# Cross attention in a decoder block: the order and size of SyncE's transfers, and preparation moved by one slot

## The chip, the cores and the metric

The kernel runs on one core of one Trainium2 chip. Times are device microseconds of one execution. Beside them one execution was taken with the hardware profiler; all rows below are of that one.

## The reference

A post-norm decoder block on x of 8 x 256 tokens x 256 features, with a context of the same shape. The part the change touches is the second of three:

```python
x = _layernorm(x + encoder(x))          # six layers of causal linear attention and an MLP
x = _layernorm(x + _L0_xattn_ref(x, ctx, ctx, ...))
x = _layernorm(x + _L0_ffn_ref(x, ...))

# _L0_xattn_ref: 16 heads of 16
q1, k1 = einsum(qh, wq1), einsum(kh, wk1); q2, k2 = einsum(qh, wq2), einsum(kh, wk2)
s1 = einsum('bshe,bthe->bhst', q1, k1) / 4;  s2 = the same of q2, k2
attn = softmax(s1) - gain * softmax(s2)
o = einsum('bhst,bthe->bshe', attn, vp)
out = normalised_per_head(o).reshape(B, S, D) @ wo.T
```

All of it is in 32-bit floats; matrix products that need it are split into a high and a low part.

## The kernel before

Encoder, cross attention and feed-forward follow each other in one program; each engine has its own instruction list, written out by hand, and they meet only in semaphores. No scheduler moves anything. In the cross attention (`cross_stage`) the work is cut into N_ALL = 64 items N: a batch b has NI = 8, for four groups of four heads and two maps (s1, s2). `slot(N)` gives b, the item's place n = 0 to 7, the next batch e = b + 1 and the previous d = b - 1. The loop body of item N, on each engine, is called slot n here.

Operands of the scores. The tile `qs` holds the queries and `ks` the keys of one batch, in two buffers, by parity of the batch. Each pair of heads takes 64 partitions, a half for each head (`a` = 0, 1), in four groups t of 16: the high, low and high parts of queries against the high, high and low parts of keys (`PARTS`: t = 0, 1, 3), and in group t = 2 a row of the negated maxima in qs against a row of ones in ks, so that the transposed scores leave PE with their maximum already subtracted. These tiles are made by way of DRAM: SP stores k_hi, k_lo to `key_rows` and q_hi, q_lo to `query_rows` (store_keys_hi, store_keys_lo, store_queries), and loads them back in the stacked layout (stack_keys, stack_queries; six loads each, of 16 partitions). stack_queries works on one half c of the heads, KC = 2 halves; stack_keys takes both halves at once. Both first write the constant rows of group 2 from the tile `unit`.

Course of an item. PE computes scores (L1272) two to three items ahead, VectorE reduces them to maxima (L1618), PE transposes these (L1279), ScalarE copies them to `mT` (L1424), and SP carries them into qs with two small DMAs (`maxima_rows`, L1146), which first wait until the item before has got its own. Then PE computes the transposed scores (L1294, two parts, pair = 0 and 1), for which it waits for those rows; ScalarE takes exp (L1447), PE multiplies by the values (L1309) and transposes every second item (L1317), VectorE normalises. scores(N + 3, 0) runs in slot N when N is odd: the first item of the next batch is met in slot 5, and it needs that batch's keys and first query half.

Preparation of batch e lies in the slots of batch b. In each slot PE does one more piece of work in the one bank `ps_j` (`side`): context transposes, x1 transposes, queries of half 0, values, queries of half 1, then the previous batch's output transposes and its two projections, in slots 0 to 7. ScalarE and VectorE empty the bank (k_hi, q_hi, values, q_lo), GpSimd normalises x1 and makes k_lo in slot 0, VectorE computes the statistics of x1 in slot 6.

SP is one in-order list: an instruction that waits holds all behind it, and its DMAs go into one queue. In slot N it does the preparation of that slot and then maxima_rows(N + 2). The preparation is: slot 1 the high keys' store; slot 2 the low ones' and the context load (256 KB each); slot 3 all of stack_keys (two constants and six loads of 128 KB) and the stores of the first query half (2 x 256 KB); slot 4 its stack (6 x 128 KB); slots 5 and 6 the same for the second half; slot 7 the input load.

## Time and profile before

| what | us |
|---|---|
| median of 3 runs | 1777.21 |
| the runs | 1775.44, 1777.21, 1781.47 |
| the profiled execution | 1771.35 |
| its span in the profile | 1769.3 |
| cross attention, first to last transposed scores | 1260.48 to 1653.20 |

The span is what the rows below are counted in; 2.05 us of the profiled execution lie outside it. The stage before (encoder) ends on PE at about 1260 us, the feed-forward follows at 1653 us. Engines are PE (matmuls), PEld (its weight loads), DVE (VectorE), ACT (ScalarE), POOL (GpSimd) and SP, whose rows, as SPq, show only the issuing of DMAs. A wait in brackets is idle time of the engine ahead of the row, with who ended it; "issue" means that the profile shows no releaser. In a view by stretch, the three last numbers are PE's granted clock as a share of full speed, the mean busy share of the 16 DMA engines, and what they moved in GB/s.

### The profile page before, as it was taken

The numbers are of one execution on the slowest core, as the hardware profiler recorded it, in microseconds if no ns is written. First come the engines' busy times: TensorE is split into PE (matmuls) and PEld (weight loads), VectorE is DVE, ScalarE is ACT, GpSimd is POOL, SyncE is SP. The second block draws the span as 40 slices with busy tenths as digits, with TensorE's granted clock in tenths as the row PEclk, the third lists the DMA queues.
The fourth block names the chain that finished last, engine by engine and source line by source line (L and its number), as shares of the span: only waits on it lengthen the run. The fifth ranks groups of instructions, "written<-read, shape, count | busy, mean of one in ns | idle before, by whom it ended". The sixth has DMA issues, their size and how long they took to land.

```text
span 1769.3 us, 38571 instructions
## 1 busy us (share of the span) xinstructions
PE 1580.0 (89%) x16078; PEld 1259.8 (71%) x16078; DVE 1254.1 (71%) x2543; ACT 957.9 (54%) x1516; POOL 784.8 (44%) x580
## 2 busy tenths in 40 slices
PE   5799999999999999999999999999856676776898
PEld 4688888888888888888888888888634444444434
DVE  4767878787877878787788778887745555654456
ACT  3455665555665655555665655554444454554445
POOL 3343555344543555344553455346323444431335
PEclk8899999999999999999999999999978888887999
DMA  6101000110010000110010000103455646444001
GB/s 117 49 1 31 7 7 23 31 31 11 25 31 27 9 8 25 31 31 11 25 31 10 22 11 25 33 2 69 91 100 96 108 86 109 86 72 68 14 1 48
DMA packets 71197, 71.55 MB, mean 40 GB/s; under 512 B 18352, under 2 KB 59248, under 8 KB 71024
## 3 DMA queue, kind: packets, MB, share of 16 engines
q1 hardware_dynamic: 71024, 69.09, 19.1%
q8 instruction: 127, 2.08, 0.5%
q14 instruction: 46, 0.38, 0.1%
HBM read 50.78 MB, written 14.68 MB: 37 GB/s over the span
## 4 chain that ended last, share of the span: by engine, by line
PE 69%; DVE 10%; SPq 6%; issue 5%; DMA 4%; ACT 4%; POOL 2%; ACTq 0%; DVEq 0%
PE e_pr L167 8%; PE e_pr L169 7%; PE e_pr L168 7%; PE e_tr L414 5%; PE e_sc L387 5%; DMA x_qs<-x_mT 3%; PE e_sc L169 3%; PE e_sc L168 3%; PE e_sc L167 3%; PE e_tr L167 3%; PE e_tr L169 3%; PE e_tr L168 3%; PE e_tr L424 2%; PE f_bank L1845 2%; PE x_psO L1309 2%
## 5 line engine op out<-in xcount | busy, mean ns | idle before, releaser
L697 POOL TENSOR_TENSOR e_h_lo<-e_h_f,e_h_hi 128x512 fp32r<-128x512 f32 x192 | 247.1, 1289 | 302.5 <-ACT e_h_hi L539 299.9
L787 DVE TENSOR_TENSOR e_am<-e_sc,c_amask 128x1024 f32<-128x1024 f32 x192 | 225.6, 1216 | 18.7 <-PE e_sc L387 18.5
L538 ACT ACTIVATE e_h_f<-e_pr,e_h_bias 128x512 f32<-128x512 f32 x192 | 132.1, 688 | 186.0 <-PE e_pr L169 182.5
L1618 DVE TENSOR_REDUCE x_mx<-x_psS 128x4 f32<-128x1024 f32 x128 | 151.5, 1219 | 112.2 <-PE x_psS L1272 112.1
L1447 ACT ACTIVATE x_ex<-x_psT 128x1024 f32<-128x1024 f32 x128 | 130.9, 1023 | 146.0 <-PE x_psT L1294 142.6
L167 PE MATMUL e_pr<-e_yT_hi,e_W_hi 128*128 128x512 f32 x384 | 168.9, 440 | 0.0
L167 PE MATMUL e_tr<-e_W_hi,e_h_hi 128*128 128x256 f32 x576 | 163.8, 284 | 0.0
L168 PE MATMUL e_tr<-e_W_lo,e_h_hi 128*128 128x256 f32 x576 | 161.6, 281 | 0.0
L169 PE MATMUL e_tr<-e_W_hi,e_h_lo 128*128 128x256 f32 x576 | 161.4, 280 | 0.0
L169 PE MATMUL e_pr<-e_yT_hi,e_W_lo 128*128 128x512 f32 x384 | 152.9, 398 | 0.0
L168 PE MATMUL e_pr<-e_yT_lo,e_W_hi 128*128 128x512 f32 x384 | 152.2, 396 | 0.0
L539 ACT ACTIVATE e_h_hi<-e_pr,e_h_bias 128x512 fp32r<-128x512 f32 x192 | 130.6, 680 | 0.0
L680 POOL TENSOR_TENSOR e_k_lo<-e_qkT,e_k_hi 128x512 fp32r<-128x512 f32 x48 | 63.7, 1348 | 143.5 <-ACT e_k_hi L548 143.5
L1294 PE MATMUL x_psT<-x_qs,x_ks 64*128 64x256 f32 x512 | 67.4, 344 | 65.2 <-DMA x_qs<-x_mT 63.1
L663 POOL TENSOR_TENSOR X<-X,e_b 128x1024 f32<-128x1024 f32 x24 | 58.1, 2421 | 134.4 <-PE e_tr L347 134.4
L167 PEld LDWEIGHTS e_tr<-e_W_hi,e_h_hi 128*128 128x128 f32 x576 | 109.2, 190 | 0.3
L169 PEld LDWEIGHTS e_tr<-e_W_hi,e_h_lo 128*128 128x128 f32 x576 | 109.1, 189 | 0.0
L168 PEld LDWEIGHTS e_tr<-e_W_lo,e_h_hi 128*128 128x128 f32 x576 | 109.0, 189 | 0.0
L414 PE MATMUL e_tr<-e_am,e_vx 128*32 128x128 f32 x3072 | 104.6, 277 | 0.0
L1272 PE MATMUL x_psS<-x_ks,x_qs 64*128 64x256 f32 x512 | 62.5, 341 | 46.2 <-issue 41.4
L1294 PEld LDWEIGHTS x_psT<-x_qs,x_ks 64*128 64x128 f32 x512 | 44.6, 213 | 82.4 <-DMA x_qs<-x_mT 67.0
L770 DVE SCALAR_TENSOR_TENSOR X<-X,e_rs,e_be 128x256 f32<-128x256 f32 x192 | 101.1, 577 | 0.0
(281 smaller groups left out, 4448.7 us busy)
## 6 DMA issues: line engine op xcount, KB each, us to landing
e_raw_m<-in_L_attn_W_dram SPq DMA_DIRECT2D x12, 1024.0 KB, 7.2
x_qs<-query_rows SPq DMA_DIRECT2D x96, 128.0 KB
x_ks<-key_rows SPq DMA_DIRECT2D x48, 128.0 KB, 5.2
query_rows<-x_q_hi SPq DMA_DIRECT2D x16, 256.0 KB, 4.9
query_rows<-x_q_lo SPq DMA_DIRECT2D x16, 256.0 KB, 5.2
x_ctok<-in_ctx_dram SPq DMA_DIRECT2D x8, 256.0 KB, 2.9
x_xo<-in_x_dram SPq DMA_DIRECT2D x8, 256.0 KB, 4.7
key_rows<-x_k_hi SPq DMA_DIRECT2D x8, 256.0 KB, 2.2
```

The costliest lines, as they stand in the source:

```text
L167: pe.matmul(out, stat[0], mov[0], start=first, stop=False)
L168: pe.matmul(out, stat[0], mov[1], start=False, stop=False)
L169: return pe.matmul(out, stat[1], mov[0], start=False, stop=last)
L414: mm = pe.matmul(out_block(s, g)[HP * a:HP * (a + 1), :], vx[:, s, h, :], am[:, s % 2, c, r, p, :], start=(s % 2 == 1 and g == 0), stop=(g ...
L538: act.activation(h_f[:, m % HR, :], ps_pr[m % 2][:, :], ACT.Gelu, bias=h_bias[:, m:m + 1])
L539: act.activation(h_hi[:, m, :], ps_pr[m % 2][:, :], ACT.Gelu, bias=h_bias[:, m:m + 1]).then_inc(gelu_done, 1)
L697: pool.tensor_tensor(h_lo[:, m, :], h_f[:, m % HR, :], h_hi[:, m, :].bitcast(F32), ALU.subtract).then_inc(h_lo_done, 1)
L770: dve.scalar_tensor_tensor(x, x, rs[i][:, s:s + 1], bias[:, :], ALU.mult, ALU.add).then_inc(ln_done[i], 1)
L787: dve.tensor_tensor(am[:, s % 2, c, :, :, :], ps_sc[:, :, c * 2 * P:(c + 1) * 2 * P].rearrange("p r (h n) -> p r h n", n=P), amask[:, :].u ...
L1294: mm = pe.matmul(ps_t[:, a, c * S:(c + 1) * S], ks[j][rows, 2 * g + pair, blk(c)], qs[j][rows, 2 * g + pair, k, :], start=True, stop=True, ...
L1447: act.activation(ex[:, N % 2, pair].rearrange("p a c n -> p (a c n)"), ps_t[:, :, :].rearrange("p a n -> p (a n)"), ACT.Exp).then_inc(ex_d ...
L1618: dve.tensor_reduce(mx[:, N % 2, :, 0:HG].rearrange("p i (a h) -> p h a i", a=2)[:, pair], ps_s[pair][:, :, :].rearrange("p a (i j) -> p a ...
```

## The change

SP now sends the rows of the maxima ahead of each slot's preparation (maxima_rows(N + 1) at the head of slot N), and the preparation is divided differently among the slots. stack_keys takes one half c of the heads (64 KB loads), and both stack functions can issue a part of their six loads (`steps`), in an order (`STACK`) that alternates the two partition halves. The constant rows are written once for each buffer, before the loop (`fixed_rows`); of the queries' only the maxima's row itself is reset from batch 2 on, as before. PE waits for the keys of a half with the queries of that half. All preparation from the context transposes on comes one slot earlier: the context of batch b + 2 is transposed in slot 7 of batch b (batch 1's before the loop), x1 in slot 0, and so on, and the output transposes always in slot 4, projections in 5 and 6. GpSimd's x1 and k_lo move to slot 7, VectorE's q_lo to slots 1 and 3, its statistics of x1 behind the maxima in slot 6.

```diff
             cross.scores(1, 1)
             cross.maxima(1)
             cross.scores(2, 0)
+            pe.wait_ge(z_done[2], SB * NT * L)
             cross.items()
...
-    LOADS = 2 * len(PARTS) + 2
+    STACK = [(a, part) for part in PARTS for a in range(2)]
...
+    def keys_arrived(n):
+        return 16 * (len(STACK) * n + 4 * min((n + 1) // 2, 2))
+
+    def queries_arrived(n):
+        return 16 * (len(STACK) * n + 2 * max(n - 2 * KC, 0))
...
-        def stack_keys(e):
-            wait(sp, t_full, 2 * NI * (e - 1))
+        def fixed_rows(e):
             sp.wait_ge(sets_done, 3)
-            wait(sp, ks_loaded, 16 * LOADS * e)
+            if e > 0:
+                sp.wait_ge(ks_loaded, keys_arrived(KC * e))
             for a in range(2):
-                sp.dma_start(ks[e % 2][half_rows(a, 2), :, :].bitcast(F32),
+                sp.dma_start(ks[e][half_rows(a, 2), :, :].bitcast(F32),
                              unit[0:DH, :].unsqueeze(1).broadcast_to([DH, PAIRS, S])).then_inc(ks_loaded, 16)
-            sp.wait_ge(k_stored, 32 * e + 32)
-            for a in range(2):
-                for t, _, low in PARTS:
-                    part = key_rows[e, low].rearrange("c (r a d) n -> a d (c r) n", a=2, d=DH)[a]
-                    sp.dma_start(ks[e % 2][half_rows(a, t), :, :].bitcast(F32), part).then_inc(ks_loaded, 16)
+                sp.dma_start(qs[e][half_rows(a, 2), :, :, :].rearrange("p r k n -> p (r k) n").bitcast(F32),
+                             unit[DH:2 * DH, :].unsqueeze(1).broadcast_to([DH, PAIRS * MAPS, S])).then_inc(ks_loaded, 16)
+
+        def stack_keys(e, c, steps=STACK):
+            n = KC * e + c
+            pairs = slice(PC * c, PC * (c + 1))
+            if steps[0] == STACK[0]:
+                wait(sp, t_full, 2 * NI * (e - 1))
+                if n > 0 and n != KC:
+                    sp.wait_ge(ks_loaded, keys_arrived(n))
+                sp.wait_ge(k_stored, 32 * e + 32)
+            for a, (t, _, low) in steps:
+                part = key_rows[e, low, c].rearrange("(r a d) n -> a d r n", a=2, d=DH)[a]
+                sp.dma_start(ks[e % 2][half_rows(a, t), pairs, :].bitcast(F32), part).then_inc(ks_loaded, 16)
...
-        def stack_queries(e, c):
+        def stack_queries(e, c, steps=STACK):
             n = KC * e + c
             pairs = slice(PC * c, PC * (c + 1))
-            wait(sp, t_full, 2 * NI * (e - 1))
-            wait(sp, qs_loaded, 16 * LOADS * n)
-            lanes = DH if e < 2 else 1
-            for a in range(2):
-                sp.dma_start(qs[e % 2][half_rows(a, 2, lanes), pairs, :, :].rearrange("p r k n -> p (r k) n").bitcast(F32),
-                             unit[DH:DH + lanes, :].unsqueeze(1).broadcast_to([lanes, PC * MAPS, S])).then_inc(qs_loaded, 16)
-            sp.wait_ge(q_stored, 32 * n + 32)
-            for a in range(2):
-                for t, low, _ in PARTS:
-                    part = query_rows[e, low, c].rearrange("(r a d) m -> a d r m", a=2, d=DH)[a]
-                    sp.dma_start(qs[e % 2][half_rows(a, t), pairs, :, :].rearrange("p r k n -> p r (k n)").bitcast(F32), part).then_inc(qs_loaded, 16)
+            if steps[0] == STACK[0]:
+                wait(sp, t_full, 2 * NI * (e - 1))
+                wait(sp, qs_loaded, queries_arrived(n))
+                for a in range(2 if e >= 2 else 0):
+                    sp.dma_start(qs[e % 2][half_rows(a, 2, 1), pairs, :, :].rearrange("p r k n -> p (r k) n").bitcast(F32),
+                                 unit[DH:DH + 1, :].unsqueeze(1).broadcast_to([1, PC * MAPS, S])).then_inc(qs_loaded, 16)
+                sp.wait_ge(q_stored, 32 * n + 32)
+            for a, (t, low, _) in steps:
+                part = query_rows[e, low, c].rearrange("(r a d) m -> a d r m", a=2, d=DH)[a]
+                sp.dma_start(qs[e % 2][half_rows(a, t), pairs, :, :].rearrange("p r k n -> p r (k n)").bitcast(F32), part).then_inc(qs_loaded, 16)
...
         load_input(0)
         load_context(1)
         store_keys_hi(0)
+        fixed_rows(0)
         store_keys_lo(0)
-        stack_keys(0)
+        for c in range(KC):
+            stack_keys(0, c)
         load_input(1)
         for c in range(KC):
             store_queries(0, c)
             stack_queries(0, c)
         maxima_rows(0)
-        maxima_rows(1)
-        load_input(2)
+        fixed_rows(1)
         for N in range(N_ALL):
             b, n, e, d, after, before = slot(N)
+            if N + 1 < N_ALL:
+                maxima_rows(N + 1)
+            if after and n == 0:
+                store_keys_hi(e)
+                store_keys_lo(e)
             if after and n == 1:
-                store_keys_hi(e)
+                stack_keys(e, 0)
+                if e + 1 < B:
+                    load_input(e + 1)
             if after and n == 2:
-                store_keys_lo(e)
+                store_queries(e, 0)
+            if after and n == 3:
+                stack_queries(e, 0, STACK[:4])
+            if after and n == 4:
+                stack_queries(e, 0, STACK[4:])
+                stack_keys(e, 1, STACK[:3])
                 if e + 1 < B:
                     load_context(e + 1)
-            if after and n == 3:
-                stack_keys(e)
-                store_queries(e, 0)
-            if after and n == 4:
-                stack_queries(e, 0)
             if after and n == 5:
                 store_queries(e, 1)
             if after and n == 6:
-                stack_queries(e, 1)
-            if n == 7 and e + 2 < B:
-                load_input(e + 2)
-            if N + 2 < N_ALL:
-                maxima_rows(N + 2)
+                stack_queries(e, 1, STACK[:4])
+            if after and n == 7:
+                stack_queries(e, 1, STACK[4:])
+                stack_keys(e, 1, STACK[3:])
...
-            if n == 0 and pair == 0:
-                pe.wait_ge(ks_loaded, 16 * LOADS * (b + 1))
             if k == 0 and pair == 0 and g % 2 == 0:
-                pe.wait_ge(qs_loaded, 16 * LOADS * (KC * b + g // 2 + 1))
+                pe.wait_ge(ks_loaded, keys_arrived(KC * b + g // 2 + 1))
+                pe.wait_ge(qs_loaded, queries_arrived(KC * b + g // 2 + 1))
...
         def side(N):
 
             b, n, e, d, after, before = slot(N)
             if after and n == 0:
-                pe.wait_ge(q_lo_done, KC * e)
-                wait(pe, z_done, QB * (b - 1))
-                context(e, ps_j)
+                x1_transpose(e, ps_j)
             if after and n == 1:
-                x1_transpose(e, ps_j)
+                queries(e, 0, ps_j)
             if after and n == 2:
-                queries(e, 0, ps_j)
-            if after and n == 3:
                 pe.wait_ge(q_lo_done, KC * e + 1)
                 values(e, ps_j)
-            if after and n == 4:
+            if after and n == 3:
                 pe.wait_ge(v_done, e + 1)
                 queries(e, 1, ps_j)
             if not after and n < 2 * KC:
@@ -1342,16 +1356,21 @@
                     pe.wait_ge(q_lo_done, KC * B)
                     pe.wait_ge(z_done, QB * (B - 2))
                 ffn.rows_in(n // KC, n % KC, ps_j)
-            if before and project_slot(n, after) == -1:
+            if before and n == 4:
                 if after:
                     pe.wait_ge(q_lo_done, KC * e + 2)
                 else:
                     ffn.rows_taken()
                 out_transpose(d)
-            if before and 0 <= project_slot(n, after) < QB:
-                out_project(d, (project_slot(n, after),))
+            if before and n in (5, 6):
+                out_project(d, (n - 5,))
+            if n == 7 and b + 2 < B:
+                pe.wait_ge(q_lo_done, KC * e + 2)
+                wait(pe, z_done, QB * b)
+                context(b + 2, ps_j)
 
         def items():
+            context(1, ps_j)
             for N in range(N_ALL):
...
             maxima(0)
             maxima(1)
+            context(1, ps_j[:, :])
...
@@ -1465,19 +1485,19 @@
                     out_copy((N - 2) // 2)
                 exps(N, 1)
                 if after and n == 0:
-                    context(e, ps_j[:, :])
+                    x1_transposed(e)
                 if after and n == 1:
-                    x1_transposed(e)
+                    queries_hi(e, 0)
                 if after and n == 2:
-                    queries_hi(e, 0)
+                    values(e, ps_j[:, :])
                 if after and n == 3:
-                    values(e, ps_j[:, :])
-                if after and n == 4:
                     queries_hi(e, 1)
                 if not after and n in (0, KC):
                     ffn.rows_in(n // KC, ps_j[:, :])
-                if before and n == (5 if after else 4):
+                if before and n == 4:
                     out_transposed(d)
+                if n == 7 and b + 2 < B:
+                    context(b + 2, ps_j[:, :])
...
         def items():
+            x1_norm(1)
+            keys_lo(1)
             for N in range(N_ALL):
                 b, n, e, d, after, before = slot(N)
-                if after and n == 0:
-                    x1_norm(e)
-                    keys_lo(e)
...
                 if n == 4 and b + 2 < B:
                     encoder_scale(b + 2)
                     encoder_add(b + 2)
+                if n == 7 and b + 2 < B:
+                    x1_norm(b + 2)
+                    keys_lo(b + 2)
...
         def items(also):
+            x1_stats(1)
             for N in range(N_ALL):
                 b, n, e, d, after, before = slot(N)
                 if N % 2 and N >= 3:
                     normalise((N - 3) // 2)
-                if N == 0:
-                    x1_stats(1)
...
                     encoder_stats(b + 2)
-                if n == 6 and b + 2 < B:
-                    x1_stats(b + 2)
                 if N in also:
                     also[N]()
                 if N + 2 < N_ALL:
                     maxima(N + 2, 1)
                 if N + 3 < N_ALL:
                     maxima(N + 3, 0)
-                if after and n == 2:
+                if after and n == 1:
                     queries_lo(e, 0, ps_j[:, :])
-                if after and n == 4:
+                if after and n == 3:
                     queries_lo(e, 1, ps_j[:, :])
                 if not after and n in (1, KC + 1):
                     ffn.rows_in(n // KC, ps_j[:, :])
-                if before and (5 if not after else 6) <= n < (7 if not after else 8):
-                    residual(d, (n - (6 if after else 5),))
+                if n == 6 and b + 2 < B:
+                    x1_stats(b + 2)
+                if before and n in (5, 6):
+                    residual(d, (n - 5,))
```

SP's list, before, in batch 1, which prepares batch 2: from the low keys' store in slot 2 to the maxima rows behind slot 4 (x_mT is the tile of the maxima, x_unit the constants; two DMAs of x_mT belong to one item):

```order
L1103 DMA key_rows<-x_k_lo 128x2x256
L1088 DMA x_ctok<-in_ctx_dram 128x2x256
L1146 DMA x_qs<-x_mT 1x2x256 x2
L1110 DMA x_ks<-x_unit 16x8x256 x2
L1116 DMA x_ks<-key_rows 16x8x256 x6
L1121 DMA query_rows<-x_q_hi 128x512
L1123 DMA query_rows<-x_q_lo 128x512
L1146 DMA x_qs<-x_mT 1x2x256 x2
L1132 DMA x_qs<-x_unit 1x8x256 x2
L1138 DMA x_qs<-query_rows 16x4x512 x6
L1146 DMA x_qs<-x_mT 1x2x256 x2
```

and after, in the same batch, from slot 1 to slot 4:

```order
L1132 DMA x_ks<-key_rows 16x4x256 x6
L1099 DMA x_xo<-in_x_dram 128x2x256
L1161 DMA x_qs<-x_mT 1x2x256 x2
L1137 DMA query_rows<-x_q_hi 128x512
L1139 DMA query_rows<-x_q_lo 128x512
L1161 DMA x_qs<-x_mT 1x2x256 x2
L1148 DMA x_qs<-x_unit 1x8x256 x2
L1153 DMA x_qs<-query_rows 16x4x512 x4
L1161 DMA x_qs<-x_mT 1x2x256 x2
L1153 DMA x_qs<-query_rows 16x4x512 x2
L1132 DMA x_ks<-key_rows 16x4x256 x3
L1095 DMA x_ctok<-in_ctx_dram 128x2x256
```

Before, ten large DMAs stand between two pairs of x_mT in slot 3 and six in slot 4; after, seven at most, with six of these (the keys of one half, in slot 1) half as large.

PE's list, before, slot 0 of batch 1 and the start of slot 1 (x_psT the transposed scores, x_psJ the bank of the side work, x_ctok the context):

```order
L1294 MATMUL x_psT<-x_qs,x_ks 128x256 x4
L1309 MATMUL x_psO<-x_ex,x_vx 32x256 x8
L1272 MATMUL x_psS<-x_ks,x_qs 128x256 x4
L1294 MATMUL x_psT<-x_qs,x_ks 128x256 x4
L1272 MATMUL x_psS<-x_ks,x_qs 128x256 x4
L1209 MATMUL x_psJ<-c_ident,x_ctok 128x128 x4
L1279 MATMUL x_psS<-c_ident,x_mx 128x128 x2
L1294 MATMUL x_psT<-x_qs,x_ks 128x256 x4
L1317 MATMUL x_psO<-c_ident,x_oS 128x128 x4
L1272 MATMUL x_psS<-x_ks,x_qs 128x256 x8
L1294 MATMUL x_psT<-x_qs,x_ks 128x256 x4
L1209 MATMUL x_psJ<-c_ident,x_x 128x128 x4
```

and after, slot 7 of batch 0 and the following slot 0:

```order
L1338 MATMUL x_psO<-c_ident,x_oS 128x128 x4
L1293 MATMUL x_psS<-x_ks,x_qs 128x256 x8
L1315 MATMUL x_psT<-x_qs,x_ks 128x256 x4
L1231 MATMUL x_psJ<-c_ident,x_ctok 128x128 x4
L1330 MATMUL x_psO<-x_ex,x_vx 32x256 x8
L1300 MATMUL x_psS<-c_ident,x_mx 128x128 x2
L1315 MATMUL x_psT<-x_qs,x_ks 128x256 x4
L1330 MATMUL x_psO<-x_ex,x_vx 32x256 x8
L1293 MATMUL x_psS<-x_ks,x_qs 128x256 x4
L1315 MATMUL x_psT<-x_qs,x_ks 128x256 x4
L1293 MATMUL x_psS<-x_ks,x_qs 128x256 x4
L1231 MATMUL x_psJ<-c_ident,x_x 128x128 x4
```

The context transposes stand one slot earlier, and the x1 transposes take their place in slot 0; around them nothing else moves.

## Rows read from the trace of the kernel before

**Rows 1.** The page, busy time of each engine and its share.
```profile
PE 1580.0 (89%) x16078; PEld 1259.8 (71%) x16078; DVE 1254.1 (71%) x2543; ACT 957.9 (54%) x1516; POOL 784.8 (44%) x580
```

**Rows 2.** PE's waits, 1260 to 1655 us: in total, times, longest.
```profile
PE x_psT L1294 <- DMA x_qs<-x_mT: 63.1, 14, 6.5
PE x_psS L1272 <- issue: 41.4, 7, 6.5
```

**Rows 3.** Busy time by stretch: batch 2 and batch 7; columns in the first line.
```profile
core 0: us, PE busy (x) PEld busy (x) DVE busy (x) ACT busy (x) POOL busy (x), PEclk, DMA share, GB/s
...
1364.48:1415.78 51.30, 35.68 (x324) 23.18 (x325) 28.52 (x52) 25.37 (x35) 21.92 (x16) 0.83 0.55 94
1621.69:1653.20 31.51, 29.66 (x279) 17.95 (x279) 20.73 (x37) 21.34 (x28) 9.88 (x6) 0.95 0.07 16
```

**Rows 4.** The same view: stores, key loads, query loads of batch 2.
```profile
1376.00:1378.00 2.00, 1.35 (x10) 0.75 (x8) 2.00 (x3) 1.24 (x3) 1.74 (x1) 1.00 0.85 252
1381.00:1387.00 6.00, 4.94 (x56) 2.85 (x52) 5.15 (x11) 4.45 (x7) 5.05 (x6) 1.00 1.01 136
1394.00:1398.00 4.00, 0.00 (x0) 0.00 (x0) 1.25 (x2) 0.00 (x0) 0.00 (x0) 0.50 1.08 127
```

**Rows 5.** Timeline, slots 2 and 3 of batch 2: start, duration, engine, line.
```profile
1373.24 0.50 PE L1294 MATMUL x_psT<-x_qs,x_ks 64*128 64x256 f32 x4
...
1373.80 1.16 SPq L1146 DMA_DIRECT2D x_qs<-x_mT  x2
...
1377.73 0.50 PE L1294 MATMUL x_psT<-x_qs,x_ks 64*128 64x256 f32 x4
...
1378.75 0.74 PE L1272 MATMUL x_psS<-x_ks,x_qs 64*128 64x256 f32 x8
```

**Rows 6.** Timeline, slots 4 and 5 of batch 2; waits in brackets.
```profile
1380.95 4.85 SPq L1116 DMA_DIRECT2D x_ks<-key_rows  x6
...
1382.24 0.50 PE L1294 MATMUL x_psT<-x_qs,x_ks 64*128 64x256 f32 x4
...
1386.84 1.31 SPq L1146 DMA_DIRECT2D x_qs<-x_mT  x2
...
1391.13 0.80 PE L1294 MATMUL x_psT<-x_qs,x_ks 64*128 64x256 f32 x4 [5.19 <-DMA x_qs<-x_mT]
```

**Rows 7.** Timeline, slots 5, 6 and 7 of batch 2.
```profile
1391.94 2.67 SPq L1138 DMA_DIRECT2D x_qs<-query_rows  x6
...
1400.18 0.80 PE L1272 MATMUL x_psS<-x_ks,x_qs 64*128 64x256 f32 x4 [6.48 <-issue]
...
1404.31 0.50 PE L1294 MATMUL x_psT<-x_qs,x_ks 64*128 64x256 f32 x4
...
1407.94 0.50 PE L1294 MATMUL x_psT<-x_qs,x_ks 64*128 64x256 f32 x4
```

**Rows 8.** Timeline, from slot 7 of batch 1 into batch 2.
```profile
1357.27 0.41 DVE L1648 TENSOR_TENSOR x_z<-x_psJ,x_x 128x256 f32<-128x256 f32 x1
...
1359.10 1.25 SPq L1146 DMA_DIRECT2D x_qs<-x_mT  x2
...
1364.48 0.50 PE L1294 MATMUL x_psT<-x_qs,x_ks 64*128 64x256 f32 x4 [3.28 <-DMA x_qs<-x_mT]
```

**Rows 9.** The page, DMA issues: KB each, us from issue to landing.
```profile
key_rows<-x_k_hi SPq DMA_DIRECT2D x8, 256.0 KB, 2.2
```

**Rows 10.** Timeline of SP's queue before batch 0.
```profile
1216.24 0.37 SPq L1099 DMA_DIRECT2D key_rows<-x_k_hi  x1
...
1223.67 1.42 SPq L1110 DMA_DIRECT2D x_ks<-x_unit  x2
```

**Rows 11.** PE's waits, 1236 to 1256 us.
```profile
PE x_psS L1272 <- DMA x_qs<-query_rows: 4.5, 1, 4.5
```

**Rows 12.** Timeline, slots 0 and 2 of batch 2.
```profile
1367.42 1.11 PE L1209 MATMUL x_psJ<-c_ident,x_ctok 128*128 128x128 f32 x4
...
1375.28 0.69 DVE L1641 TENSOR_REDUCE x_om<-x_sq 128x32 f32<-128x512 f32 x1 [1.65 <-POOL x_sq L1534]
```

2 lines of the change are left out of this document (removed).

## Prediction

> **What bounds the kernel now.** I read the page first: PE is busy 89% of the span [rows 1], so the question is where the remaining time is lost. The list of PE's waits in the cross attention (1260 to 1655 us) names two kinds of long wait and hardly anything else: 63.1 us in 14 waits of the transposed scores for the rows of the maxima, and 41.4 us in 7 waits of at most 6.5 us in front of the scores, labelled "issue" [rows 2]. Two and one, so three to a batch, for seven batch boundaries (0/1 to 6/7). The third reading is by batch: batch 2 goes from 1364.48 to 1415.78 us, 51.3 us, with PE busy 35.7 us at a granted clock of 0.83; the last batch, for which nothing is prepared, takes 31.5 us for the same eight slots, at 0.95 [rows 3]. The fourth is the DMA rate: loads that stack rows into qs or ks run at 127 to 136 GB/s with the DMA engines' share at 1.0, while a store with the context load reaches 252 GB/s [rows 4]. So a 128 KB stacking load takes 1.0 us, however deep the queue, and a 256 KB store or context 1.04 us.
>
> An undisturbed slot is the measure for everything below [rows 5]. Slot 2 starts at 1373.24, SP issues the rows of the maxima 0.56 us later in two DMAs (1.16 us), slot 3 starts at 1377.73: 4.49 us, no DMA wait. I take 4.4 us as a slot, a tenth less because VectorE waits in slot 2 for something that moves (below). The rows issued early in slot N are needed at the start of slot N+1, so they have 8.8 us counted from the start of slot N-1, whose preparation is what lies ahead of them in the queue.
>
> The three stalls, seen in one batch: **Into slot 5.** Slot 3 queues 1 MB of key loads and constants and then 0.5 MB of query stores. The key loads alone keep SP until 1385.80; with slot 4 begun at 1382.24 it could have sent the rows at 1382.8, sends them at 1386.84, and they land behind the backlog: slot 5 starts at 1391.13, PE idle 5.19 us [rows 6]. **Within slot 5.** PE's scores of the next batch's first item need that batch's first query stack; its six loads are only issued from 1391.94, and PE stands 6.48 us until 1400.18 [rows 7]. **Into the next batch.** The rows wait behind 0.75 MB of the second query stack: sent at 1359.10, slot 0 starts at 1364.48, PE idle 3.28 us [rows 8]. That is 14.95 us of 51.3.
>
> **The change part by part.**
>
> *The order "maxima first" alone: nothing.* maxima_rows(N+1) ahead of slot N's preparation is the same cyclic order as maxima_rows(N+2) behind it. What differs is what lies between two pairs of rows.
>
> *The packets.* Per batch SP now puts in: slot 0, both key stores (2.1 us of queue time); slot 1, six 64 KB key loads and the input (3 + 1 = 4); slot 2, two stores (2.1); slot 3, four query loads (4); slot 4, two query loads, three 64 KB key loads and the context (2 + 1.5 + 1 = 4.5); slot 5, two stores (2.1); slot 6, four loads (4); slot 7, two and three (3.5). Sum 26.3 us, in eight slots of 4.4 = 35.2. A key store takes 2.2 us from issue to landing [rows 9], 1.04 of it data, so data begins 1.2 us after issue. In slot 3: rows sent at 0.56, done at 1.72, two small constant DMAs (1.4 us of issue, as the pair in [rows 10]), data from 4.3 to 8.3; the next rows land at about 8.4, needed at 8.8. Slot 4's queue starts at 8.4 - 4.4 = 4.0: its two query loads end at 6.0, that is 1.6 us into slot 5, and the scores of the next batch want them at about 1.4 (in slot 3 the eight scores matmuls begin at 1378.75, 1.0 after its start, and the second four are meant) [rows 5]. Then keys and context to 8.5, rows at 8.6, needed at 8.8. Slot 6 is slot 3 again, with 0.4 us to spare, and less if slot 6 itself is short (3.63 us in the trace, 1404.31 to 1407.94 [rows 7]). Slot 1 ends at 2.9 + 4 = 6.9. So the three stalls go, but with 0.2 to 0.4 us of margin in three places and some 0.2 missing in one. I leave a rest of 1.0 us a batch; its bounds are 0 and, if every one of the four loaded slots is late by 1 us, 4 us.
>
> *Constants written once.* The 16 unit rows of ks (two loads of 128 KB) vanish from each batch: 2 us less of the queue, in slot 3, where it counts; contained in the sum above. For both buffers they are now sent before the loop, 768 KB each. The first set fills a gap: after the store of the high keys at 1216.24 SP has nothing to issue until the low ones are there, and starts the constants at 1223.67 [rows 10]. The first query stack had four constants of 128 KB ahead of it in the queue, so it arrives some 4 us earlier, and PE's wait of 4.5 us for it [rows 11] all but goes. The second set goes out behind the first maxima rows, 6 us of queue; the second rows, needed one slot (4.6 us) after slot 0 begins, just clear it. I count 3.5 us of gain, between 0 and 4.5, with the next edit taken off.
>
> *Preparation one slot earlier.* The PE items keep their number, eight a batch, one in each slot; each is preceded by the one it was preceded by before, so no new neighbour in bank psJ. The context transposes of batch 1 (1.11 us, [rows 12]) move in front of slot 0 and are paid openly, 1 us once, since slot 0 has one item again (x1). New waits: PE's context in slot 7 waits for the residual of slot 6; queued behind it are attend and the transposed maxima. In the trace VectorE ran the residual of slot 6 at 1357.27 (0.41 us), at the very start of slot 7 [rows 8]; the x1 statistics now stand in front of it, so it ends about 1.9 us into slot 7, and PE comes to its context at 2.0 to 2.2: nothing, at worst 0.3 us a batch. GpSimd normalises x1 behind it, until about the slot's end, before PE's x1 transposes 2 us into slot 0. VectorE's q_lo moves from slots 2 and 4 to 1 and 3, which also hold the normalisation; it sits in a gap before the next maxima, so nothing. In slot 2 VectorE stood 1.65 us, until 1375.28, for GpSimd's squares [rows 12], which run behind x1 and the low keys that now lie in slot 7: 0.5 us a batch of that I take as gain (0 to 0.9).
>
> *What stalls leave behind.* Without its wait slot 5 lasted 13.18 - 6.48 = 6.7 us, at half clock and with every engine starting cold; slots 4 and 6 were short in exchange (3.70 and 3.63). Against 4.4 each that nets 2.3 - 0.7 - 0.8 = 0.8 us a batch.
>
> **The sum.** A batch: 51.3 - 14.95 - 0.8 - 0.5 + 1.0 = 36.1 us, 15.2 less. Seven of them 106.4, and 3.5 at the start: 110 us. The profiled execution took 1771.35 us (span 1769.3), so 1661; it was 5.9 us under the median of the runs, 1777.21, so the median should come to 1667 us.
>
> A rule against the interleaving of halves, and a row: one key stack of six loads ran at 136 GB/s although consecutive loads in it go to different groups of 16 partitions [rows 4]; so alternating halves won't be faster than that and I give it nothing. The Trainium skill, "DMA: Bandwidth & Descriptors", Rules for kernel authors, says the same of two transfers to disjoint halves: they serialize. Its page "SBUF — State Buffer", on the port swizzle, gives bandwidth by how many of 16 ports the partitions reach; 16 partitions reach four, an estimate of 109 GB/s (the rows show somewhat more), and two halves eight. By that rule loads in flight together could go twice as fast, the rest of 1.0 us a batch would be gone, and the sum would give 1660; the trace speaks for the first.
>
> **The rivals.**
> 1. *The rows stay late in loaded slots.* For it: the margins above are a few tenths, and SP's issues sometimes take longer with a deep queue. Against: 26 us of 35 are used. 4 to 8 us a batch, 28 to 56 in all, less the 7 counted: 1688 to 1716, say 1700.
> 2. *The slots themselves become shorter.* Slots of the last batch took 31.5/8 = 3.94 us at a clock of 0.95 [rows 3]; half way to it (4.17, no rest) is 33.4 a batch, 19 us more gained: 1648.
> 3. *Each added DMA costs its start.* Twelve key loads instead of six; if the 1.2 us before data [rows 9] did not overlap, 7.2 us a batch, 50 us: 1717. Against: in rows 4 six loads follow each other at a share of 1.01. The skill's page on DMA (Anatomy of one DMA) puts about 2.0 us fixed on each; paid in line that would be 84 us and 1751; no row shows it paid in line.
> 4. *No gain.* The waits reappear in other slots, as many in sum, since PE then waits for each pair of rows: 8 x 1.9 us. That needs a queue that is never empty; 9 us a batch are free. 1775.
> 5. *Slower.* The smaller, alternating loads run much slower than 1.0 us per 128 KB. The queue decides from the point where a batch's DMA time passes 51.3 us: 8.3 us of other work and 18 units of load at 2.4 us. At 2.9 us it is 60.5 us, 9.2 more, seven times: 1842. Against: 1 KB rows of keys and 2 KB rows of queries ran alike [rows 4].
>
> **How the numbers follow.** Forecast 0.60 (1655 to 1688), rival 1 0.20, rival 2 0.12, rival 3 0.03, rival 4 0.02, rival 5 0.03. The range that holds 8 in 10 takes the forecast's, most of rival 2 and half of rival 1: 1645 to 1702. A measurement of this kernel tells 0.3%, 5 us, from no change. Faster by more: 0.60 + 0.20 + 0.12 + 0.03 = 0.95; same 0.02; slower 0.03.
>
> **What would show it.** Right: PE's waits for the maxima rows under 10 us in all (63.1 now), its "issue" waits in front of the scores under 7 us (41.4), batches 35 to 37 us apart, clock above 0.93 over the stage, no PE wait for the first query stack. Rival 1: many waits of 1 to 2 us for the maxima rows, slots 3, 4 and 6. Rival 2: batches near 33 us. Rivals 3 and 5: gaps in the DMA share, or a rate under 100 GB/s, within a stack. Wrong altogether: a new line high in PE's waits, such as the context behind x_z.

## The result, and the profile after

| kernel | median, us | runs | against before | 95% interval |
|---|---|---|---|---|
| before | 1777.35 | 1775.44 to 1781.47 | | |
| after | 1679.96 | 1677.79 to 1681.22 | 0.9448 | 0.9428 to 0.9468 |

The change saves 97 us, 5.5%. The profiled execution after took 1678.82 us, its span is 1677.1; the span before was 1769.3, so 92.2 us of span are to be found. The forecast was 1667 (1661 for the profiled execution, 110 us less); the time lies within 1645 to 1702, 13 us above the forecast.

The page first. Same work, as many instructions on each engine, but less busy time on PE than in [rows 1]:

```profile
PE 1566.9 (93%) x16078; PEld 1251.7 (75%) x16078; DVE 1259.3 (75%) x2543; ACT 957.5 (57%) x1516; POOL 784.8 (47%) x580
```

PE's waits in the cross attention (1255 to 1600 us; total, times, longest), to be laid beside [rows 2]:

```profile
PE x_psT L1315 <- DMA x_qs<-x_mT: 18.3, 14, 2.6
...
PE x_psS L1300 <- DVE x_mx L1640: 6.7, 17, 1.3
PE x_psO L1330 <- DVE x_o L1655: 3.9, 7, 0.7
PE x_psJ L1231 <- POOL x_x L1540: 2.9, 1, 2.9
PE x_psS L1293 <- DMA x_ks<-key_rows: 1.7, 2, 1.1
```

The 63.1 us for the rows of the maxima are 18.3, in as many places (14) but none over 2.6 us. The 41.4 us of "issue" in front of the scores are gone without a trace. New, and small, are a wait for x_o in each slot 7 and one for x_x in the first slot.

By stretch (us, busy time and count of PE, PEld, DVE, ACT, POOL, then clock, DMA share, GB/s): batches 2 and 7 after, as [rows 3], then batches 1 to 6 together, after and, in the second fence, before.

```profile
1339.70:1377.64 37.94, 33.37 (x324) 21.32 (x324) 29.50 (x54) 25.26 (x35) 22.00 (x17) 0.96 0.60 121
1529.10:1560.10 31.00, 29.48 (x279) 18.39 (x279) 20.56 (x35) 21.43 (x28) 9.98 (x5) 0.94 0.12 21
1303.83:1529.10 225.27, 199.08 (x1940) 127.59 (x1940) 173.44 (x301) 150.91 (x209) 119.68 (x86) 0.95 0.55 120
```

```profile
1313.16:1621.69 308.53, 216.50 (x1944) 139.41 (x1944) 169.48 (x300) 151.97 (x210) 119.45 (x86) 0.83 0.53 92
```

Six batches take 83.3 us less, 13.9 each. Of these, 17.4 us are PE's own busy time (216.5 to 199.1 for the same matmuls), since the granted clock rose from 0.83 to 0.95 when the long waits went; the other 65.8 are idle time. The rest of the 92.2: batch 0 is 11.4 shorter (52.7 to 41.3 us), the last batch 0.5, but the first transposed scores come 2.0 us later (1262.52 for 1260.48), and what follows the last transposed scores takes 0.9 more (117.0 for 116.1). 83.3 + 11.4 + 0.5 - 2.0 - 0.9 = 92.3.

All of this is one execution of each kernel. A second profiled execution of the same kernel (after_again, below) has 38.5 us for batch 0 in place of 41.3 and 38.1 in place of 37.5 for each of the next six, so the mean of the six is known to some 0.6 us, and batch 0 only to 3 us.

Where the remaining waits stand: timeline of slots 3 to 5 of batch 2 (slot 3 begins at 1351.46).

```profile
1352.27 1.18 SPq L1161 DMA_DIRECT2D x_qs<-x_mT  x2
...
1353.54 1.36 SPq L1148 DMA_DIRECT2D x_qs<-x_unit  x2
...
1354.94 1.84 SPq L1153 DMA_DIRECT2D x_qs<-query_rows  x4
1356.01 0.51 PE L1315 MATMUL x_psT<-x_qs,x_ks 64*128 64x256 f32 x4
...
1356.89 1.22 SPq L1161 DMA_DIRECT2D x_qs<-x_mT  x2
...
1361.96 1.18 SPq L1161 DMA_DIRECT2D x_qs<-x_mT  x2
1361.99 0.50 PE L1315 MATMUL x_psT<-x_qs,x_ks 64*128 64x256 f32 x4 [2.27 <-DMA x_qs<-x_mT]
```

The rows issued at 1356.89 stand behind four query loads. My working gave the loads' data until 8.3 us after the slot's start, 1359.8, and the rows right behind. The four 1 KB packets of these rows were in fact moved from 1359.34 to 1359.60, a little earlier than that. But PE saw them at 1361.96, 2.3 us later: their last completion is recorded at 1361.94. In a slot without loads ahead it is complete 0.3 us after its packets (rows issued at 1352.27, packets 1353.47 to 1354.17, last completion 1354.46). The loads themselves are as late: the fourth one's last packet ended at 1359.55, its last completion came at 1361.27, 1.7 us later, and the rows' came next. This is no single case. There are fourteen places in this trace where rows stand behind four loads; in twelve of them the completion came 1.7 to 2.3 us after the rows' packets, in the other two 0.5 and 1.0. So a small transfer behind such loads into 16 partitions pays not only for their data but, in most places, also for a landing of some 2 us after its own packets. I had put 0.1 us there.

The wait costs a second time, in slot 5. That slot lasts 6.0 us (1361.99 to 1368.00), where the last batch has 4.5 for it, and there is no long wait inside it. PE works in it at half clock for a part of the time:

```profile
1364.50:1366.60 2.10, 2.10 (x9) 1.27 (x12) 2.10 (x3) 1.02 (x1) 0.43 (x1) 0.50 0.72 265
```

The start: SP's queue after, to be laid beside [rows 10], and PE's wait of [rows 11] as it is now.

```profile
1217.89 0.37 SPq L1106 DMA_DIRECT2D key_rows<-x_k_hi  x1
1218.62 0.78 SPq L1117 DMA_DIRECT2D x_ks<-x_unit  x1
...
1220.82 2.12 SPq L1119 DMA_DIRECT2D x_qs<-x_unit  x1
1224.89 0.36 SPq L1110 DMA_DIRECT2D key_rows<-x_k_lo  x1
1228.42 7.04 SPq L1132 DMA_DIRECT2D x_ks<-key_rows  x12
...
1239.55 3.13 SPq L1153 DMA_DIRECT2D x_qs<-query_rows  x6
```

```profile
PE x_psS L1293 <- DMA x_qs<-query_rows: 4.3, 1, 4.3
```

The constants filled the gap and ran over it: 768 KB from 1218.62 on, the last landed at 1228.17. The low keys' store, issued behind them, landed at 1228.41, and everything after it (twelve key loads, 7 us of issue, with a wait between the halves; query stores; query loads) is late by as much as the constants were to save. The wait is 4.3 us where it was 4.5. Of the 2.0 us by which the stage begins later, 1.65 are there before any of this: the high keys' store went out at 1217.89, at 1216.24 before [rows 10], behind an encoder that the change doesn't touch. Counted from that store the first transposed scores come after 44.6 us, 44.2 before: no gain, and the loss is 0.4.

### The profile page after: what moved, and what is told of

Read it like the earlier page. It is cut to its first block, busy times and chain, and to the rows that moved or that the text cites. A ratio compares the mean times of both kernels' runs of the same rounds, so it can differ in the third digit from the quotient of the medians.

```text
span 1677.1 us, 38614 instructions
## 1 busy us (share of the span) xinstructions
PE 1566.9 (93%) x16078; PEld 1251.7 (75%) x16078; DVE 1259.3 (75%) x2543; ACT 957.5 (57%) x1516; POOL 784.8 (47%) x580
## 4 chain that ended last, share of the span: by engine, by line
PE 73%; DVE 10%; SPq 5%; DMA 4%; ACT 4%; issue 3%; POOL 1%; ACTq 0%; DVEq 0%; POOLq 0%
PE e_pr L167 8%; PE e_pr L169 7%; PE e_pr L168 7%; PE e_tr L414 6%; PE e_sc L387 5%; PE e_sc L167 3%; PE e_sc L168 3%; PE e_sc L169 3%; PE e_tr L167 3%; PE e_tr L169 3%; PE e_tr L168 3%; DMA x_qs<-x_mT 3%; PE e_tr L424 3%; PE x_psO L1330 2%; PE f_bank L1866 2%
## 5 line engine op out<-in xcount | busy, mean ns | idle before, releaser
L167 PEld LDWEIGHTS e_pr<-e_yT_hi,e_W_hi 128*128 128x128 f32 x384 | 72.5, 189 | 32.4 <-issue 13.9
L764 DVE SCALAR_TENSOR_TENSOR X<-X,e_mv,e_g 128x256 f32<-128x256 f32 x192 | 93.1, 544 | 0.0
L414 PEld LDWEIGHTS e_tr<-e_am,e_vx 128*32 128x32 f32 x3072 | 78.6, 110 | 15.6 <-issue 12.3
```

What stands on the lines that cost most here:

```text
L167: pe.matmul(out, stat[0], mov[0], start=first, stop=False)
L414: mm = pe.matmul(out_block(s, g)[HP * a:HP * (a + 1), :], vx[:, s, h, :], am[:, s % 2, c, r, p, :], start=(s % 2 == 1 and g == 0), stop=(g ...
L764: dve.scalar_tensor_tensor(x, x, mv[i][:, s, 0:1], gain[:, :], ALU.subtract, ALU.mult).then_inc(xc_done[i], 1)
```

## The experiments

Twelve kernels. Times are medians; the ratio is to the kernel before on the same chip (1773 to 1777 us). "Rows wait" is PE's wait for the maxima's rows in the cross attention (total / places); "batches" is the mean of batches 1 to 6.

| run | us | ratio, interval | rows wait | batches |
|---|---|---|---|---|
| after | 1679.96 | 0.9448, 0.9428 to 0.9468 | 18.3 / 14 | 37.5 |
| after_again | 1678.25 | 0.9469, 0.9450 to 0.9487 | 18.9 / 13 | 38.1 |
| q_half | 1646.09 | 0.9277, 0.9248 to 0.9306 | 3.3 / 6 | 33.1 |
| tail_quarter | 1669.07 | 0.9405, 0.9373 to 0.9436 | 14.4 / 15 | 36.1 |
| split33 | 1669.09 | 0.9404, 0.9381 to 0.9428 | 7.4 / 13 | 36.6 |
| stats_first | 1676.89 | 0.9445, 0.9417 to 0.9472 | 23.6 / 15 | 37.8 |
| unsplit | 1713.31 | 0.9673, 0.9656 to 0.9689 | 45.6 / 16 | 43.0 |
| half_major | 1685.99 | 0.9515, 0.9498 to 0.9531 | 24.1 / 16 | 39.0 |
| act_queue | 1710.89 | 0.9654, 0.9639 to 0.9670 | 9.8 / 11 | 42.5 |
| const_spread | 1671.68 | 0.9407, 0.9393 to 0.9422 | 19.8 / 17 | 37.8 |
| reset_early | 1654.34 | 0.9308, 0.9294 to 0.9323 | 4.7 / 7 | 34.5 |
| before_const | 1764.43 | 0.9927, 0.9909 to 0.9945 | 47.6 / 14 | 49.9 |
| combined | 1643.64 | 0.9268, 0.9246 to 0.9290 | 3.8 / 7 | 33.6 |

### Less data in the queue: q_half and tail_quarter

```diff
+                some = slice(PC * c, PC * c + (2 if e > 1 else PC))
-                sp.dma_start(qs[...][half_rows(a, t), pairs, :, :]..., part)
+                sp.dma_start(qs[...][half_rows(a, t), some, :, :]..., part[:, 0:some.stop - some.start, :])
```

What isn't loaded stays stale, so q_half leaves out half of the queries' data. In tail_quarter the 2 is a 1, and the condition holds only for the last two loads of a stack.

> The changed kernel, but from batch 2 on each of the six query loads brings two of its four pairs of heads, 64 KB in place of 128 KB (the rest of the queries is stale). The queue's time in slots 3 and 6 falls from 4 to 2 us. Theory A, that the maxima rows wait for the loads ahead of them in the queue (drained) plus some 2 us until those writes are acknowledged: PE's waits for the maxima rows (18.3 us in all in the changed kernel) fall under 4 us for batches 2 to 7, a batch takes 34 to 35 us in place of 37.7, the kernel 1660 to 1664. Theory B, that something else than the queue makes slots 4, 5 and 7 long (VectorE's order, half clock): batches stay above 36.5 us, 1675 or more.

> The changed kernel, but from batch 2 on the last two query loads of each half, issued in slots 4 and 7 behind the maxima rows, bring one pair of heads in four, 32 KB in place of 128 KB (the rest is stale). What lies ahead of the maxima rows is untouched. Theory A (rows held by what is ahead of them, and 2 us of late acknowledgement): PE's wait at the start of slot 5 stays at 1.5 to 2.5 us a batch and the one at the next batch's start near 1 us; only slot 5 itself gets shorter (6.0 to 5.0), 1672 to 1677. Theory C (rows held by the loads sent behind them, which fill the same ports until they have landed): both waits go, 1664 to 1669.

With half the bytes of the query loads of batches 2 to 7 (0.75 MB less for each) 15 of the 18.3 us of waiting go and a batch takes 33.1 us: 34 us less in all, 27 of them in batches 1 to 6, more than expected. With only the last two loads cut, slots 4 and 7 are relieved by 1.5 us each, but 14.4 us of waits stay in 15 places, as Theory A has it. The time, 1669, does not fit A (1672 to 1677); it lies at the end of what C gave (1664 to 1669), though C's sign, that both waits go, failed. So the loads in slots 3 and 6, ahead of the rows, seem to count for most, and those behind them for a part. Neither run says whether data or landing is the larger part.

### Other cuts of the same data: split33 and unsplit

```diff
             if after and n == 3:
-                stack_queries(e, 0, STACK[:4])
+                stack_queries(e, 0, STACK[:3])
             if after and n == 4:
-                stack_queries(e, 0, STACK[4:])
-                stack_keys(e, 1, STACK[:3])
+                stack_queries(e, 0, STACK[3:])
...
             if after and n == 5:
                 store_queries(e, 1)
+                stack_keys(e, 1, STACK[:3])
             if after and n == 6:
-                stack_queries(e, 1, STACK[:4])
+                stack_queries(e, 1, STACK[:3])
             if after and n == 7:
-                stack_queries(e, 1, STACK[4:])
+                stack_queries(e, 1, STACK[3:])
```

> The changed kernel with the six query loads of a half divided 3 and 3 instead of 4 and 2 over slots 3/4 and 6/7, and the first three key loads of the second half moved from slot 4 to slot 5. Theory A: one load less ahead of the rows, so the waits at slot 5 and at the next batch lose 1 us each, slot 5's wait for the stack stays; 1.5 to 2 us a batch, 1668 to 1671. Theory C: one load more behind the rows, so these waits grow by up to 1 us: 1680 to 1690.

At 3 us of loads in each slot in place of 4 the rows' waits fall from 18.3 to 7.4 us, none over 1.5. But the third load of the second part now arrives after the scores that need it: PE's waits list has a line that after does not have.

```profile
PE x_psS L1293 <- issue: 9.3, 7, 2.1
```

These waits (9.3 us) are nearly what the rows' have lost (10.9), and still the kernel is 10.9 us faster; a part of that is PE's own time, 197.0 us at a clock of 0.97 in batches 1 to 6, where it was 199.1 at 0.95. The opposite, in unsplit: `stack_keys(e, 0)` and `stack_keys(e, 1)` whole in slot 1, `stack_queries` whole in slots 3 and 6.

> The changed kernel with its preparation one slot earlier, its constants written once and its rows first, but the loads undivided: both halves' key loads (twelve of 64 KB) together in slot 1, the six query loads of a half whole in slots 3 and 6. Only the division of the loads is undone. My theory (a slot's queue must leave some 2 us beside its data, since the rows land 2 us after their packets): slots 1, 3 and 6 each queue 6 us of loads (slot 1 with the input 7) in a slot of 4.4, so each makes the rows late by 2 to 4 us; waits for the rows of the maxima 7 x 7 us, about 50 in all against 18.3 now, batches 41 to 43 us, 1705 to 1720. Rival (the order of the rows and the constants are what pays, a division within the load phase is worth little because the queue drains in the light slots): batches 38 to 39 us, 1680 to 1690.

```profile
PE x_psT L1311 <- DMA x_qs<-x_mT: 45.6, 16, 5.1
```

1713 us and 45.6 us of waits, as the late landing said (1705 to 1720, about 50). So dividing the loads is worth 2.0 to 2.3 of the 5.5%; the other 3.3% come from rows first, preparation one slot earlier and constants once, together. In this run too there is no wait of the scores for queries, and in before_const (next) they all stay, so it was neither the division nor the keys' constants that removed those 41.4 us.

### One cost by itself: before_const

```diff
-            wait(sp, ks_loaded, 16 * LOADS * e)
-            for a in range(2):
+            wait(sp, ks_loaded, keys_arrived(e))
+            for a in range(2 if e < 2 else 0):
                 sp.dma_start(ks[e % 2][half_rows(a, 2), :, :]..., unit[0:DH, :]...)
```

> The kernel before with one part of the change alone: the unit rows of ks (two loads of 128 KB) go out only with the first key stack of each buffer, not in slot 3 of every batch. My sum had counted them at 2 us of queue in slot 3. Theory: slot 3's backlog is 2 us shorter from batch 1 on, and the two waits in slot 5 both stand at its end, so six batches get 2 us shorter: 12 us, a ratio of 0.993. Rival (the query stack of slot 4 takes over: its start is set by the stores, not by the keys): no change, 0.998 to 1.002.

0.9927: 13 us by the ratio, 12.2 by the two medians (1776.61 and 1764.43), where 12 were expected. By the spans it is 6.4 us, but the profiled execution of before was a fast one, 6.0 under its median, so the medians are the better measure. The scores' "issue" waits stay, and the rows' shrink from 63.1 by 15.5, not all of which reaches the time, since PE is busy 222.1 us in batches 1 to 6 at a clock of 0.81, where it was 216.5 at 0.83. PE's waits from 1260 to 1655 us:

```profile
PE x_psT L1297 <- DMA x_qs<-x_mT: 47.6, 14, 5.8
PE x_psS L1275 <- issue: 41.8, 7, 6.5
```

### Who is late in slot 7: stats_first

```diff
                     encoder_stats(b + 2)
+                if n == 6 and b + 2 < B:
+                    x1_stats(b + 2)
                 if N in also:
...
-                if n == 6 and b + 2 < B:
-                    x1_stats(b + 2)
                 if before and n in (5, 6):
```

> The changed kernel with VectorE's statistics of x1 put back ahead of the maxima of slot 6, as they stood before the change. If the new place costs (PE waits 3.9 us in 7 waits for VectorE's x_o in slot 7, 0.2 us in 1 wait before): those waits go and slot 7 gets 0.5 us shorter, 1675 to 1678. Rival: the maxima of slot 6 come 1.3 us later and slot 6 pays what slot 7 gets: 1679 to 1682.

In after VectorE runs the x1 statistics and then the residual at the start of slot 7, ahead of the normalisation that PE waits for:

```profile
1372.26 0.74 DVE L1606 BATCH_NORM_STATS2 x_st<-x_xw 128x6 f32<-128x256 f32 x2
...
1373.40 0.42 DVE L1670 TENSOR_TENSOR x_z<-x_psJ,x_x 128x256 f32<-128x256 f32 x1
...
1374.47 0.60 DVE L1655 SCALAR_TENSOR_TENSOR x_o<-x_tmp,x_neg_gain 128x128 f32<-128x128 f32 x1
...
1375.22 1.07 PE L1330 MATMUL x_psO<-x_ex,x_vx 128*32 128x256 f32 x16 [0.68 <-DVE x_o L1655]
```

With the statistics ahead of the maxima the wait for x_o falls from 3.9 us to 0.5, and the one for the rows rises from 18.3 to 23.6. The median of 1676.9 lies where the theory had it, but it can't be told from that of after (0.9445 against 0.9448 and 0.9469), and the waits side with the rival. The wait had cover: whoever passes PE's x_o earlier stands for the rows longer.

### The order within a stack: half_major

```diff
-    STACK = [(a, part) for part in PARTS for a in range(2)]
+    STACK = [(a, part) for a in range(2) for part in PARTS]
```

> The changed kernel with one edit: the six loads of a stack go first to the three groups of one half, then to those of the other, in place of alternating (the cuts after four, two and three loads stay where they are). My theory (loads in one queue run one after the other at 127 to 136 GB/s whichever partitions they go to): same time within 0.3%, 1680. Rival (two loads to different halves of the partitions overlap and share more of the write side, so alternating them is what makes them fast): each stack loses a tenth to a half of its rate, 0.4 to 2 us in each of four loaded slots, 11 to 50 us in all, and the DMA share and GB/s in the stretches of the loads fall.

> The changed kernel itself once more, so that the other kernels have it beside them on the same chip: 0.945 of the kernel before, within 0.3%; waits for the rows of the maxima about 18 us in some 14 places.

1686 us, ratio 0.9515 against 0.9469 on the same chip: 0.5% slower, with intervals that just do not touch, and 24.1 us of waits for 18.9. My theory (no difference) is wrong by a little. In the load phase of slot 3, batch 2, the same 3.5 us (from 4.0 to 7.5 after the slot's start), first after, then half_major:

```profile
1355.46:1358.96 3.50, 3.50 (x46) 2.10 (x38) 3.12 (x9) 2.72 (x4) 1.52 (x3) 1.00 0.87 141
```

```profile
1351.07:1354.57 3.50, 3.50 (x46) 2.10 (x38) 3.12 (x9) 2.72 (x4) 1.52 (x3) 1.00 0.92 135
```

Over these windows of batches 1 to 6 the mean is 147 and 141 GB/s, single ones lie between 134 and 159 and between 118 and 155. So two loads to different halves in flight together gain some 4% at most by this measure, which is less than the spread of the windows, and not the double that the prediction works out from ports. The Trainium skill, "DMA: Bandwidth & Descriptors", Rules for kernel authors, has them serialize, and the trace agrees up to these 4%.

### Another queue for the rows: act_queue

```diff
             copy(mT[0:HG, N % 2, :], ps_s[1][0:HG, 0, 0:S], mT_tr, N + 1, mT_done)
...
+            if n == 0:
+                act.wait_ge(ks_loaded, keys_arrived(KC * b + 1))
+            if k == 0 and g % 2 == 0:
+                act.wait_ge(qs_loaded, queries_arrived(KC * b + g // 2 + 1))
+            wait(act, rows_set, 32 * N)
+            act.wait_ge(mT_done, N + 1)
+            for a in range(2):
+                act.dma_start(qs[b % 2][HALF * a + DH * 2:HALF * a + DH * 2 + 1, 2 * g:2 * g + 2, k, :].bitcast(F32),
+                              mT[2 * a:2 * a + 2, N % 2, :].bitcast(F32)).then_inc(rows_set, 16)
...
-        maxima_rows(0)
...
-            if N + 1 < N_ALL:
-                maxima_rows(N + 1)
```

> The changed kernel with the rows of the maxima issued by ScalarE into its own DMA queue, right behind its copy of the transposed maxima, instead of by SyncE; all loads and stores stay in SyncE's queue. Theory A1 (rows land late because they stand in one queue behind loads, each waiting for the completion of the one before): in a queue of their own they land within 2 us of issue whatever SyncE has queued; waits for the rows fall from 18 us to under 5, batches 35 to 36 us, though ScalarE pays about 0.9 us of issue in each slot, which it has (it is busy half the time); about 1665. Rival A2 (the lateness sits in the DMA engines, which serve all queues: the rows' packets and write receipts share them with the loads): waits stay at 10 to 18 us, time 1675 to 1685. Rival A3 (ScalarE's issue time, and its wait for earlier rows, hold up the exps): waits of PE for x_ex or for maxima appear, 1685 or more.

1711 us. The third case decides the time: ScalarE's issue stands between the copy and the exp, and PE pays for it in every slot. With slots that much longer, the 9.8 us of waits for the rows can't decide between the first two (under 5, or 10 to 18).

```profile
PE x_psT L1303 <- ACT x_ex L1465: 66.6, 80, 2.5
PE x_psT L1303 <- DMA x_qs<-x_mT: 9.8, 11, 1.6
```

What the run was for can be read all the same, in slots 3 to 5 of batch 2, ScalarE's issues and PE's wait:

```profile
1375.24 1.16 ACTq L1460 DMA_DIRECT2D x_qs<-x_mT  x2
...
1381.82 0.50 PE L1303 MATMUL x_psT<-x_qs,x_ks 64*128 64x256 f32 x4 [1.36 <-DMA x_qs<-x_mT]
```

In a queue of their own, with nothing ahead of them in it, the rows take 6.5 us, since SyncE's six query loads had been issued just before. Their four packets (1 KB, in the second queue) moved from 1378.91 to 1379.84, from 3.7 us after the issue on, and their last completion came at 1381.78, 1.9 us after the packets. So the lateness doesn't come from the order within one queue; it lies in what both queues share, and its second part is the completion. The Trainium skill, "DMA: Bandwidth & Descriptors", Queues, rings and completion order, states that the increment of a semaphore is a strongly ordered write, which lands only after every earlier write of that DMA engine, across its queues. That fits both this run and after: the last of SyncE's query loads was complete at 1380.96 here and at 1361.27 there, and the rows' completions came next, up to 1381.78 and 1361.94. The rule itself no run here shows apart from other causes.

### The constants: const_spread

```diff
-        fixed_rows(0)
+        fixed_keys(0)
+        fixed_queries(0, 0)
         store_keys_lo(0)
-        for c in range(KC):
-            stack_keys(0, c)
+        stack_keys(0, 0)
+        store_queries(0, 0)
+        fixed_queries(0, 1)
+        stack_queries(0, 0)
+        stack_keys(0, 1)
         load_input(1)
-        for c in range(KC):
-            store_queries(0, c)
-            stack_queries(0, c)
+        store_queries(0, 1)
+        fixed_keys(1)
+        stack_queries(0, 1)
         maxima_rows(0)
-        fixed_rows(1)
+        fixed_queries(1, 0)
```

`fixed_rows` is cut into its keys' part and one part for each half of the queries; fixed_queries(1, 1) goes out in slot 2 of batch 0.

> The changed kernel with the constant rows sent in pieces: of buffer 0 only 512 KB (keys both halves, queries one half) in the gap ahead of the low keys' store, the last 256 KB behind the first query stores; the second key stack of batch 0 behind the first query stack; buffer 1's in three pieces (256 KB each) behind the second query stores, behind the first maxima rows, and in slot 2. Theory (the early wait of 4.3 us for the first query stack stayed because 768 KB of constants overran a gap of 4.7 us, and batch 0's slots 0 and 1 are 7.2 us each because the second 768 KB stand in front of the rows and the key stores): the wait falls to under 1.5 us, slots 0 and 1 of batch 0 to 4 to 5.5 us; 3 for the wait and 4 for the slots, 7 us in all, 1671. Rival (the wait is set by the chain query stores, landing, loads, whose start the low keys and PE's own work set, not by the constants): the wait stays over 3 us and slot 0 over 6; 1676 to 1680.

Half right. PE's wait for the first query stack is gone (a wait of 1.7 us for keys stands in its place), the first transposed scores come at 1256.79 instead of 1262.52 (40.6 us behind the high keys' store instead of 44.6, so 4.1 of the 5.7 us belong to the edit), and the time is 1672 us, 0.9407 against 0.9448 and 0.9469. But slots 0 and 1 of batch 0 are as long as before this edit, 7.21 and 6.83 us, although no constants stand in front of the rows. In slot 0 it is another wait:

```profile
1260.04 2.43 POOL L1548 TENSOR_SCALAR x_x<-x_xw,x_mv,x_rs 128x256 f32<-128x256 f32 x2
...
1262.52 1.11 PE L1239 MATMUL x_psJ<-c_ident,x_x 128*128 128x128 f32 x4 [2.36 <-POOL x_x L1548]
```

Batch 1's x1 is now transposed in slot 0, and GpSimd normalises it only after VectorE's last statistics of the encoder. Slot 1 is long for another reason. It holds no long wait, but PE does its work in it at half clock:

```profile
1269.74:1276.87 7.13, 7.02 (x40) 3.99 (x39) 4.44 (x7) 3.17 (x5) 0.00 (x0) 0.50 0.41 129
```

This is slot 1 in after. In q_half, whose instructions are the same up to here, the clock was 0.82 in it and it took 4.78 us. So the wait in slot 0 costs up to 2.4 us more behind it, in some executions. The late x1 is a cost of the shift which I had not seen: I had costed it for the batches in the middle, where GpSimd has slot 7 for it, and batch 1 has no slot 7 ahead of it. The edit also puts the keys' second stack behind the first query stack, so how much of the earlier start is due to the constants isn't separated here.

### Two tiny DMAs: reset_early

```diff
             if after and n == 2:
                 store_queries(e, 0)
+                reset_maxima(e, 0)
...
             if after and n == 5:
                 store_queries(e, 1)
+                reset_maxima(e, 1)
```

`reset_maxima` is what stood at the head of stack_queries: two waits and the two DMAs from `unit`.

> The changed kernel with one step moved: the two small DMAs that reset the maxima's row in qs (8 KB each, 1.4 us of issue) go out behind the query stores of slots 2 and 5 instead of ahead of the query loads in slots 3 and 6. Same bytes, same packets. Theory (what makes the rows late in slots 4 and 7 is where the load phase ends, plus 2 us of landing): the loads' data start and end 1.4 us earlier, slots 4 and 7 shorten by 1.0 to 1.4 us in the six batches that have resets; 12 to 15 us less, 1663 to 1666, waits for the rows from 18 to about 7. Rival (SyncE's issue isn't what sets the start of the loads; the stores' landing does, or the slot in which the time is saved passes it to slot 5): under 5 us, 1675 to 1680.

The clearest run. The same packets but for the place of four 8 KB transfers a batch, and the time falls from 1679 to 1654 us (0.9308), more than the 12 to 15 expected. Slots 3 and 4 of batch 2 (slot 3 begins at 1346.21):

```profile
1347.02 1.22 SPq L1165 DMA_DIRECT2D x_qs<-x_mT  x2
...
1348.28 1.81 SPq L1157 DMA_DIRECT2D x_qs<-query_rows  x4
...
1351.32 1.17 SPq L1165 DMA_DIRECT2D x_qs<-x_mT  x2
...
1354.40 0.50 PE L1322 MATMUL x_psT<-x_qs,x_ks 64*128 64x256 f32 x4
```

The loads are issued 2.07 us after the slot's start, 3.48 in after, and the wait of 2.27 us is none. Over the stage, and over batches 1 to 6:

```profile
PE x_psT L1322 <- DMA x_qs<-x_mT: 4.7, 7, 1.0
```

```profile
1299.69:1506.51 206.82, 192.24 (x1942) 122.94 (x1942) 171.37 (x296) 151.47 (x209) 120.03 (x85) 0.99 0.59 130
```

Waits for the rows of 14.2 us are gone (18.9 in after_again, 4.7 here), somewhat more than the 11 expected. The rest of the excess is PE's own time: for batches 1 to 6 it is busy 192.2 us at a clock of 0.99, against 201.9 at 0.94 in after_again, 9.7 us less. These batches are 21.8 us shorter (228.7 and 206.8), so 12.1 of that are idle time; the spans differ by 25.4 (1677.7 and 1652.3). For each us of waiting that went, PE's busy time fell by some 0.8 us with it.

### What the runs point to: combined

The edits of const_spread, reset_early and stats_first, the context load from slot 4 to slot 5, and for batch 1:

```diff
             for s in range(SB):
                 cross.maxima(s // 2, s % 2)
+                if s == SB - 1:
+                    cross.x1_stats(1)
...
             cross.encoder_add(1)
+            cross.x1_norm(1)
             rsqrt(2, ve_done[2], NT * L)
```

Both had been the first line of their engine's `items`.

> The changed kernel with what the runs so far point to, all of it complete: the constant rows in pieces; the resets of the maxima's row behind the query stores of slots 2 and 5; the context load from slot 4 to slot 5; VectorE's statistics of batch 1's x1 ahead of the last residual of the encoder and GpSimd's normalisation of it ahead of the encoder's last power, in place of the head of the item loops; VectorE's later x1 statistics ahead of slot 6's maxima. If landing time behind full load phases was the limit, each part adds up, since the queue now has slack: resets alone gave 1652 in span; constants 5; x1 of batch 1 without PE's wait of 2.9 and slots 0 and 1 near 5 in place of 7.2, 4; slot 5 without the context 0.8 in six batches, 5; waits for x_o 3: 1635 in span, about 1637, a ratio of 0.922. Rival (as with the statistics alone, a wait taken away in one place comes back as a wait for the rows): 1648 to 1655.

1643.64 us, 0.9268: the fastest of all, 2% under after, 130 us under before, with nothing left out. It lies between the two expectations. What was said of batch 1 holds: slots 0 and 1 take 4.79 and 4.78 us, the wait for x_x is gone. What wasn't foreseen is that the keys come late in place of the rows:

```profile
PE x_psS L1311 <- DMA x_ks<-key_rows: 5.2, 7, 1.2
PE x_psT L1333 <- DMA x_qs<-x_mT: 3.8, 7, 0.9
```

```profile
1291.12:1492.92 201.80, 190.02 (x1941) 121.70 (x1940) 170.94 (x296) 150.91 (x210) 119.18 (x84) 1.00 0.56 134
```

PE is busy 190.0 of 201.8 us, 94%, at the full clock; the queue holds it up for only some 9 us in the whole stage. The five edits were taken together, so what each is worth beside the others isn't known.

## Why the prediction was nearly right

*What bounds the kernel, and that it goes.* Right. The three stalls of a batch (14.95 us) were the cost, and the two kinds of wait fell from 104.5 us to 18.3. The clock over batches 1 to 6 is 0.95, the batches 35.9 to 39.0 us; "35 to 37" was too narrow. Of the five signs that were to show it right, two held (no "issue" waits in front of the scores, clock above 0.93) and three failed: waits for the rows under 10 us (18.3), batches of 35 to 37, no wait for the first query stack (4.3). That the time came within 13 us is in part luck: errors below pull both ways.

*The order alone, nothing; the constants, 2 us of queue a batch.* The second is shown by before_const (13 us for 12; the interval is 0.55% to 0.91% of the time). The first was not tried alone.

*A rest of 1.0 us a batch.* This is the step that was mis-sized. It had the data of each slot's queue right (8.3 us, and the packets moved 8.1 after the slot's start), but took "the next rows land at about 8.4" from it. They land some 2 us after their packets when loads into 16 partitions are in front, at 10.5 in the slot shown. The waits measured 18.3 us, 2.6 a batch instead of 1.0; the margins of 0.2 to 0.4 us were no margins. The rows that I had taken the landing from could not show it: a key store's 2.2 us [rows 9] are 1.2 of start and 1.04 of data, but nothing stands ahead of it. The trace of before has it in another place, which I had quoted for its length alone: in [rows 8] the rows stand behind six query loads; 369 of the loads' 384 packets had ended by 1362.62 (the last at 1363.84), and the rows were complete at 1364.44. Rival 1 (rows late in the loaded slots, waits of 1 to 2 us in slots 3, 4 and 6) was true in kind, at a third of its price. What the rest of 1.0 us left out besides is the clock: a wait of 2.3 us is followed by a slot 5 partly at half clock, and reset_early shows some 0.8 us of PE's time for each us of waiting.

*Preparation one slot earlier: nothing, at worst 0.3 a batch.* Waits for x_o of 3.9 us in seven slots 7, which stats_first shows to be covered by those for the rows; and for batch 1's x1, once, slots 0 and 1 of 7.2 and 7.1 us where they had been 4.6 and 5.5, which nothing in the prediction held. const_spread took away the cause that I had suspected, and it stayed; combined took away this one as well, and it went. So batch 0 gained 11.4 instead of 15.2 (14.2 by the second execution).

*Slots of 4.4 us.* Slots 0 and 2 of most batches are now 3.63 us, where I kept 4.4 in slot 0 and took 0.5 off in slot 2. Rival 2 was true for these two slots, and they made up for part of the rest. In all a batch in the middle gained 13.9 us, not 15.2.

*3.5 us at the start.* Failed. The wait of 4.5 us stayed at 4.3, and the stage began 2.0 us later, 0.4 of it by the change. I had summed what the queue no longer carries ahead of the first queries, and not asked when the constants themselves end. The low keys' store went out 6.3 us after the first constants; 768 KB at the 1.0 us per 128 KB that the prediction itself used, behind its 1.2 us before data, take 7.2, and 9.6 were measured to the last landing (1218.62 to 1228.17). const_spread supports it: with 512 KB in the gap, and six key loads behind the first query stack, the stage begins 4.1 us earlier, counted from the high keys' store.

Together: 7 x 15.2 + 3.5 = 110 forecast; 11.4 + 83.3 + 0.5 at the end - 2.0 - 0.9 = 92 measured. Of the 18 us between, 7.9 lie in the batches 1 to 6, 3.8 in batch 0, 5.5 at the start (1.65 of these the encoder's), 0.4 behind batch 6.

*Interleaving the halves: nothing.* It is worth 0.5%, 8 us (half_major against after_again). The 1660 that the prediction works out from ports did not come. The step from the number of ports to "twice as fast" for loads in flight together was the prediction's own, and no row had shown it.

*Rivals 3 to 5.* None came. Twelve key loads instead of six show no start paid in line: in slot 1 of batch 2 the six of 64 KB are complete 0.4 to 0.6 us after each other (from 1347.21 to 1349.66). The 2.0 us of rival 3 are the figure that the Trainium skill, "DMA: Bandwidth & Descriptors", Anatomy of one DMA, gives for transfers that GpSimd issues; these are SyncE's.

Open: what the order alone is worth and what the shift by one slot alone (unsplit and before_const leave these two as what removed the 41.4 us of "issue" waits, and don't part them); whether the 2 us of landing depend on the 16 partitions or only on the bytes ahead; a small transfer behind the same bytes into more partitions was not run.

## What to carry to other kernels

Count a queue's length to the last completion, not to the last byte, and leave 2 us of it free in every period in which loads like these stand in front of a small transfer that someone waits for; then look for what merely delays the start of the load phase, since moving four 8 KB transfers a batch gave 25 us where another division of the loads gave 10. A gap in a queue is as long as the time until the next thing that matters in it: what is put in must fit at the measured rate, its start and landing included. And when work is moved one period ahead, look at the first period by itself, which has none before it.

## What was not expected of the hardware

- A small transfer behind loads into 16 partitions each is complete some 2 us after its own packets (1.7 to 2.3 us in twelve of fourteen places in after, as 1359.60 to 1361.94), in an idle queue 0.3 us after them (1354.17 to 1354.46); and in another engine's queue it is as late (packets until 1379.84, complete at 1381.78).
- PE's time for the same matmuls of six batches is 216.5, 201.9, 199.1, 192.2 and 190.0 us at granted clocks of 0.83, 0.94, 0.95, 0.99 and 1.00: from after_again to reset_early 12.1 us of idle time went in these batches, and 9.7 us of busy time with it. No single wait for the rows was longer than 2.6 us in after, and the clock still fell to half behind them.
- Alternating between two halves of the partitions gained 0.5% of the time; the rate of the loads rose from 141 to 147 GB/s on average of six windows that spread more than that.
- The issue of two DMAs takes ScalarE 1.16 us of its own time, and 1.2 us in each slot were enough to make a kernel 2% slower, on an engine that is busy 57% of the span.
